# Value matmuls in blocks of four steps, two steps behind the scores, in a fused attention and expert layer

## The reference

```python
query = jnp.concatenate([q_nope, q_pe], axis=-1)
key = jnp.concatenate([k_nope, jnp.broadcast_to(k_pe, (B, H, S, ROPE))], axis=-1)
scores = jnp.einsum('bhsd,bhtd->bhst', query, key) * scale
attn = jax.nn.softmax(scores.astype(jnp.float32), axis=-1).astype(query.dtype)
out = jnp.einsum('bhst,bhtd->bhsd', attn, v)
```

## Time and profile before

| Stretch or engine | us |
|---|---|
| median of the timed runs | 2569.87 |
| span of the profiled execution | 2588.1 |
| TensorE busy in the span | 2303.3 (89%) |
| VectorE, ScalarE, GpSimd busy | 1390.3, 1375.7, 1380.6 |
| preparation, start to about | 178 |
| side work of head 0 alone, to about | 268 |
| attention loop, to about | 1896 |
| output projection, routing, experts, sum, to | 2588 |

### The profile page before, as it was taken

The page is one execution under the profiler, slowest core; times in us unless marked ns, Lnnn a source line. Parts: engine busy times, 40 slices in busy tenths (PEclk is TensorE's granted clock), DMA queues, the critical chain, the costliest instruction groups (busy, mean ns, idle before and its releaser), DMA issues. The chain is left out here.

```text
span 2588.1 us, 38846 instructions
## 1 busy us (share of the span) xinstructions
PE 2303.3 (89%) x10836; PEld 1411.5 (55%) x10836; DVE 1390.3 (54%) x2685; ACT 1375.7 (53%) x1915; POOL 1380.6 (53%) x810
## 2 busy tenths in 40 slices
PE   6887999999999999999999999999984565999980
PEld 3633555555555555555555555555563343777760
DVE  4527657567565575575665755756036224333327
ACT  3510566666666666666666666666832111333336
POOL 1000566666666766666666666666841464333331
PEclk9885899999999999999999999999995677999995
DMA  4216000000000000000000000000001564999978
GB/s 146 72 54 211 1 1 1 1 1 1 1 1 1 1 1 1 1 1 1 1 1 2 1 1 1 1 1 1 1 1 34 185 212 151 371 355 356 355 252 289
DMA packets 97037, 198.44 MB, mean 77 GB/s; under 512 B 13662, under 2 KB 59656, under 8 KB 96648
## 3 DMA queue, kind: packets, MB, share of 16 engines
q1 hardware_dynamic: 85384, 165.16, 19.0%
q0 software_dynamic: 11520, 31.52, 3.2%
HBM read 142.00 MB, written 54.64 MB: 76 GB/s over the span
## 5 line engine op out<-in xcount | busy, mean ns | idle before, releaser
L636 POOL TENSOR_TENSOR prob_lo<-prob,prob_hi 128x1024 f16<-128x1024 f32 x512 | 1118.1, 2185 | 591.9 <-ACT prob_hi L656 591.6
L654 ACT ACTIVATE prob<-p_s,prob_scale 128x1024 f32<-128x1024 f32 x512 | 570.6, 1114 | 622.3 <-PE p_s L806 622.3
L691 DVE TENSOR_REDUCE maxes<-p_m 128x1 f32<-128x512 f32 x1024 | 693.0, 690 | 292.5 <-PE p_m L775 282.9
L656 ACT ACTIVATE prob_hi<-p_s,prob_scale 128x1024 f16<-128x1024 f32 x512 | 566.9, 1107 | 0.0
L775 PE MATMUL p_m<-k_hi,q_hi 96*128 96x512 f32 x1024 | 443.4, 446 | 15.9 <-DVE maxes L691 12.3
L806 PE MATMUL p_s<-q_hi,k_hi 97*128 97x512 f32 x1024 | 371.8, 444 | 8.3 <-DVE q_hi L700 8.3
L806 PE MATMUL p_s<-q_lo,k_hi 97*128 97x512 f32 x1024 | 321.8, 395 | 0.0
L806 PE MATMUL p_s<-q_hi,k_lo 97*128 97x512 f32 x1024 | 321.0, 395 | 0.0
L775 PEld LDWEIGHTS p_m<-k_hi,q_hi 96*128 96x128 f32 x1024 | 194.9, 194 | 182.2 <-DVE maxes L691 134.3
L1510 PE MATMUL p_g<-w,rT 128*128 128x352 f32 x640 | 230.1, 484 | 39.1 <-issue 24.8
L806 PEld LDWEIGHTS p_s<-q_hi,k_hi 97*128 97x128 f32 x1024 | 175.5, 190 | 124.0 <-issue 110.0
(11 more groups left out here) (217 smaller groups left out, 2145.9 us busy)
## 6 DMA issues: line engine op xcount, KB each, us to landing
w<-in_experts SPq DMA_DIRECT2D x144, 608.0 KB
expert_rows<-zeros SPq DMA_DIRECT2D x64, 257.0 KB, 5.0
rows<-expert_rows SPq DMA_DIRECT2D x128, 128.5 KB
got<-ranked_out SPq DMA_DIRECT2D x16, 768.0 KB, 5.4
wqb<-in_wqb SPq DMA_DIRECT2D x16, 341.0 KB, 3.0
rows<-expert_rows SPq DMA_DIRECT2D x32, 128.0 KB
shared_out<-y SPq DMA_DIRECT2D x32, 128.0 KB
got<-shared_out SPq DMA_DIRECT2D x16, 256.0 KB, 7.1
```

Of the source, the lines that this page charges most:

```text
L636: gp.tensor_tensor(prob_lo[s % 4][:, :], prob[s % 2][:, :], prob_hi[s % 4][:, :], ALU.subtract).then_inc(lo_ready, 1)
L654: act.activation(prob[s % 2][:, :], p_s[s % 2][:, :], ACT.Exp, bias=prob_scale[:, :], scale=SCALE)
L656: act.activation(prob_hi[s % 4][:, :], p_s[s % 2][:, :], ACT.Exp, bias=prob_scale[:, :], scale=SCALE).then_inc(p_ready, 1)
L691: v.tensor_reduce(maxes[:, n:n + 1], p_m[n % 2][:, :], AX.X, ALU.max).then_inc(max_used, 1)
```

## The change

- `weigh` is issued for four steps at once. A head is eight groups; group g first issues the scores of steps 4g + 2 to 4g + 5, then `weigh` of steps 4g to 4g + 3. Scores of steps 32 and 33 are steps 0 and 1 of the next head. Before the first head, scores of steps 0 and 1 are issued by themselves.
- All side work lies at one of twelve slots of a group, one behind each part of the scores. Projections stand in the last slot of groups 0 to 3, maxima in groups 1 to 7 (8, 10, 10, 10, 10, 10, 6), turns in slot 4 of groups 0 and 4, rows 0 and 1 in slots 3 and 7 of group 6, rows 2 and 3 together in the last slot of group 7. Nothing but the four `weigh` stands between the last slot of a group and the first of the next.
- prob_hi and prob_lo have eight tiles instead of four.
- maxneg is reduced in two halves, each as soon as its 32 maxima are there; rows 0 and 1 wait for the first half only.
- c_hi and c_lo are made at the end of the keys' section in `mods_and_weights`, on VectorE, instead of at the start of `attention`.

```diff
+NB = 8
...
+            step(v.tensor_scalar(c_hi[:, :], caug[:, :], C_SCALE, None, ALU.mult))
+            v.scalar_tensor_tensor(out=c_lo[:, :], in0=caug[:, :], scalar=C_SCALE, in1=c_hi[:, :], op0=ALU.mult,
+                                   op1=ALU.subtract)
...
-        prob_hi = [sb(f"prob_hi{n}", 2 * QC, F16) for n in range(4)]
-        prob_lo = [sb(f"prob_lo{n}", 2 * QC, F16) for n in range(4)]
-        c_hi = sb("c_hi", T * CP, F16)
-        c_lo = sb("c_lo", T * CP, F16)
+        prob_hi = [sb(f"prob_hi{n}", 2 * QC, F16) for n in range(NB)]
+        prob_lo = [sb(f"prob_lo{n}", 2 * QC, F16) for n in range(NB)]
...
-        MAXIMA = (0, 0, 0, 0, 3, 4, 0, 2, 3, 3, 3, 4, 0, 2, 3, 4, 0, 2, 3, 3, 3, 3, 3, 3, 3, 3, 3, 3, 1, 0, 0, 0)
-        PROJECT = (1, 5, 11, 15)
-        assert sum(MAXIMA) == 4 * T and all(sum(MAXIMA[:s + 2]) <= 16 * c for c, s in enumerate(PROJECT))
-
-        def beside(first, last):
-
-            at = {}
-            for s in range(STEPS):
-                copy, turn, others, maxima = [], [], [], []
-                if s == 17 or (s == 1 and not first):
-                    copy = [("copy", 0 if s == 17 else 1)]
-                if s == 19 or (s == 3 and not first):
-                    turn = [("turn", 0 if s == 19 else 1)]
-                if not last:
-                    maxima = [("max", n) for n in range(sum(MAXIMA[:s]), sum(MAXIMA[:s + 1]))]
-                    others = [("project", c) for c in range(4) if PROJECT[c] == s]
-                    others += [("row", c) for c in range(4) if 28 + c == s]
-                at[s] = maxima[:2] + copy + maxima[2:] + turn + others
+        HEAD_USES = [("turn", 1), ("project", 0), ("project", 1), ("project", 2), ("project", 3), ("turn", 0),
+                     ("row", 0), ("row", 1), ("row", 2), ("row", 3)]
+        MAXIMA = (0, 8, 10, 10, 10, 10, 10, 6)
+        assert sum(MAXIMA) == 4 * T
+
+        def maxima_at(group):
+
+            first = sum(MAXIMA[:group])
+            count = MAXIMA[group]
+            at = [[] for _ in range(12)]
+            begin, end = {1: (4, 12), 7: (0, 6)}.get(group, (0, 12))
+            for n in range(count):
+                at[begin + n * (end - begin) // max(count, 1)].append(first + n)
             return at
 
+        def aside(group, slot, first, last):
+
+            if group == 0 and slot == 4 and not first:
+                return [("turn", 1)]
+            if group == 4 and slot == 4:
+                return [("turn", 0)]
+            if last:
+                return []
+            if group < 4 and slot == 11:
+                return [("project", group)]
+            if group == 6 and slot in (3, 7):
+                return [("row", slot // 4)]
+            if group == 7 and slot == 11:
+                return [("row", 2), ("row", 3)]
+            return []
+
...
-                if n == 4 * T - 1:
+                if n % (2 * T) == 2 * T - 1:
+                    half = n // (2 * T)
                     v.wait_ge(max_used, 64 * g + n + 3)
-                    v.tensor_reduce(maxneg[:, :], maxes[:, :].rearrange("p (t c) -> p t c", c=4), AX.X, ALU.max,
-                                    negate=True).then_inc(neg_ready, 1)
-                    v.wait_ge(neg_ready, g + 1)
+                    v.tensor_reduce(maxneg[:, half * 8:(half + 1) * 8],
+                                    maxes[:, half * 32:(half + 1) * 32].rearrange("p (t c) -> p t c", c=4), AX.X,
+                                    ALU.max, negate=True).then_inc(neg_ready, 1)
+                    v.wait_ge(neg_ready, 2 * g + half + 1)
...
-                v.wait_ge(o_mm, STEPS * h + 16 * half + 16 + 4)
+                v.wait_ge(o_mm, STEPS * h + 16 * half + 16 + NB)
...
+                for group in range(8):
+                    if group == 0 and not first:
+                        copy_out(1, h - 1)
+                    if group == 4:
+                        copy_out(0, h)
+                    at = maxima_at(group)
+                    for slot in range(12):
+                        if not last:
+                            for n in at[slot]:
+                                maximum(n, h + 1)
+                        for what in aside(group, slot, first, last):
+                            kind, c = what
+                            use = x_use(h, what, first, last)
+                            if kind == "project":
+                                project(c, h + 1, 1 - u, use)
+                            elif kind == "row":
+                                row(c, 1 - u, use)
+                            else:
+                                turn(c, h - c, use)
...
-            def scores(s, h, u, first, between):
+            def scores(part, s, h, u, rows_use):
 
                 half, kt = s // 16, s % 16
-                n = STEPS * h + s
-                if kt == 0:
-                    pe.wait_ge(x_used, x_base(h, first) + 2 * half - 1)
-                pe.wait_ge(p_ready, n + 1)
+                if part == 0:
+                    if kt == 0:
+                        pe.wait_ge(x_used, rows_use + 2 * half + 2)
+                    pe.wait_ge(p_ready, STEPS * h + s + 1)
                 keys = slice(kt * P, (kt + 1) * P)
-                for part, (kk, qq) in enumerate(((k_hi, q_hi), (k_hi, q_lo), (k_lo, q_hi))):
-                    if part and between:
-                        between.pop(0)()
-                    for j in range(2):
-                        c = 2 * half + j
-                        last = pe.matmul(p_s[s % 2][:, j * QC:(j + 1) * QC], kk[0:KS, keys],
-                                         qq[u][0:KS, c * QC:(c + 1) * QC], start=(part == 0), stop=(part == 2))
-                last.then_inc(s_mm, 1)
+                kk, qq = ((k_hi, q_hi), (k_hi, q_lo), (k_lo, q_hi))[part]
+                for j in range(2):
+                    c = 2 * half + j
+                    last = pe.matmul(p_s[s % 2][:, j * QC:(j + 1) * QC], kk[0:KS, keys],
+                                     qq[u][0:KS, c * QC:(c + 1) * QC], start=(part == 0), stop=(part == 2))
+                if part == 2:
+                    last.then_inc(s_mm, 1)
...
-                for s, todo in beside(first, last).items():
-                    maxima = [(lambda c=c: maximum(c, h + 1, 1 - u)) for kind, c in todo if kind == "max"]
-                    scores(s, h, u, first, maxima)
-                    if s >= 2:
-                        weigh(s - 2, h)
-                    elif not first:
-                        weigh(STEPS - 2 + s, h - 1)
-                    for m in maxima:
-                        m()
-                    for what in todo:
-                        kind, c = what
-                        if kind == "project":
-                            project(c, h + 1, 1 - u, x_use(h, what, first, last))
-                        elif kind == "row":
-                            row(c, h + 1, x_use(h, what, first, last))
-                        elif kind == "turn":
-                            turn(c, h - c, x_use(h, what, first, last))
+                own = x_use(None, ("row", 1)) if first else x_use(h - 1, ("row", 1), False)
+                for group in range(8):
+                    at = maxima_at(group)
+                    for slot in range(12):
+                        s, part = 4 * group + 2 + slot // 3, slot % 3
+                        if s < STEPS:
+                            scores(part, s, h, u, own)
+                        elif not last:
+                            scores(part, s - STEPS, h + 1, 1 - u, x_use(h, ("row", 1), first))
+                        if not last:
+                            for n in at[slot]:
+                                maximum(n, h + 1, 1 - u)
+                        for what in aside(group, slot, first, last):
+                            kind, c = what
+                            use = x_use(h, what, first, last)
+                            if kind == "project":
+                                project(c, h + 1, 1 - u, use)
+                            elif kind == "row":
+                                row(c, h + 1, use)
+                            else:
+                                turn(c, h - c, use)
+                    for s in range(4 * group, 4 * group + 4):
+                        weigh(s, h)
...
+            for s in range(2):
+                for part in range(3):
+                    scores(part, s, 0, 0, x_use(None, ("row", 1)))
```

More of the change, by code:

```diff
@@ L100, in program @@
             weff = sb(att, "weff", DK * H * KA)
-            caug = sb(att, "caug", T * CP)
+            c_hi = sb(att, "c_hi", T * CP, F16)
+            c_lo = sb(att, "c_lo", T * CP, F16)
             cosq = sb(att, "cosq", S)
@@ L518, in _, with attention @@
                 last.then_inc(ov_mm, 1)
-def attention(nc, hT, weff, caug, cosq, sinq, k_hi, k_lo, ident, slots_dram, cbar):
+def attention(nc, hT, weff, c_hi, c_lo, cosq, sinq, k_hi, k_lo, ident, slots_dram, cbar):
     st = ExitStack()
@@ L608, in x_use @@
```

(31 more changed lines are left out.)

24 lines of the change are left out of this document (9 added, 15 removed).

## The result

The changed kernel took 2586.45 us (median of four runs, 2582.96 to 2591.39) against 2567.91 us for the kernel before on the same chip: ratio 1.0078, with a 95% interval of 1.0057 to 1.0098. The forecast was 2583 us, with slower as the likeliest outcome (0.39).

The account below looks back on a forecast made before the run. TensorE's own queue order was taken to bound the attention loop. Transitions saved were expected to go into waits: 2569.9 + 8.4 (fifteen heads) + 5.3 (last head) = 2583 us, range 2528 to 2620.

Parts of the forecast that it names:

- The saving: In each head, three of four transitions between score and value matmuls go: 24 x 0.32 = 7.7 us.
- The chain of two score buffers: In a bare group, the third and fourth score steps wait for ScalarE's reading: 10.2 us instead of 9.44.
- VectorE after a projection: Behind the projections, L684 waits 0.2 to 1.0 us for GpSimd, once; the third maximum of the next group is late.
- Two rows in succession: Group 7: rows sharing one PSUM tile, row 3 starts 1.9 us after row 2 instead of 0.96; group takes 13.6.
- Group 6: Group with ten maxima and two rows inside the scores: TensorE bound, full gain, 12.7 us against 13.72.
- The head: Sum over eight groups: 102.65 us against 102.09, +0.56 a head, +8.4 us in the 15 heads with maxima.
- the missing 0.6 I leave on both sides: Per head, what the summed 102.1 us lacks against 102.7 measured, taken as equal in both kernels.
- The last head: Seven bare groups in the last head, each 0.76 us slower: +5.3 us.
- TensorE bound: Attention loop: TensorE stays bound or nearly, 2536 us, or 2448 if all waits are absent; chance 0.32.
- All three instructions blocked: After each projection, L684, L685 and L686 each wait for a whole GpSimd instruction: 2810 us; chance 0.15, nearly all at lower price.
- its milder form: After projections in four groups, one wait for GpSimd of up to 2.15 us instead of 0.2 to 1.0: +72, 2655 us.
- The 0.32 stays in the block: Value block: the 0.32 us belongs to value matmuls or their waits, not the transition; 2705 us at most; chance 0.05.

Follow-up runs that it names:

- the last kernel: Changed kernel with rows 2 and 3 apart, score buffer freed after its first reading, TensorE's loop written out and maxima placed again: 2472.47 us, ratio 0.9636.
- blocks of two: Changed kernel with weigh issued for two steps at once instead of four: 2672.2 us, ratio 1.0403; with side work placed for it 2553.75 us, ratio 0.9852.

## Why the prediction was right, and what it missed

**The saving.** Predicted: three of four transitions go, 7.7 us a head. With most waits taken away (the last kernel) a head is 97.05 against 102.07 of the kernel before without its loop, 5.0 less, and TensorE still waits 0.7 of it (10.4 us in fifteen heads). 0.4 more went back into rows (group 6 below). The remaining 1.6 or so of the 7.7 is not accounted for. In two of its groups the saving is there in full: group 5 (twelve maxima) takes 11.3 and group 3 (ten and a projection) 12.55, where the old order's prices give 12.27 and 13.49, 0.95 less each against the 0.96 of three transitions. Right in kind and, where nothing waits, in size.

**The chain of two score buffers.** Predicted: c waits 0.9 in a bare group, which takes 10.2 instead of 9.44. Measured 10.17 and waits of 0.84 and 0.35. Freeing the buffer one instruction earlier gives 9.26, so the cause is shown and not only the size.

**VectorE after a projection.** Predicted 0.9 to 1.7 us for the one instruction, and the two behind it unchanged: measured 0.75 to 1.47 (median 0.985), and 423 and 688 ns for the others. That the third maximum is late in groups 2 to 4 was shown by moving it. I had group 2 at 13.6 (13.44), group 4 at 13.2 (12.97): 0.16 and 0.23 too much.

**Two rows in succession.** Predicted a gap of about 0.9 and 13.6 for the group; 0.79 and 13.54, and 12.18 with the rows apart.

**Group 6.** Predicted 12.7, "full gain"; measured 13.17, with no wait in it. The price of a row, 0.96, was read where a value matmul stood ahead of it and scores behind it, so that it changed kinds there anyway. Now it stands inside the scores, and the timeline of after shows that it brings transitions of its own:

```profile
1085.25 0.40 PE L792 MATMUL p_m<-k_hi,q_hi 96*128 96x512 f32 x1
1085.58 1.03 PE L799 MATMUL p_x<-ident,maxneg 128*1 128x128 f32 x8
1086.54 0.72 PE L821 MATMUL p_s<-q_lo,k_hi 97*128 97x512 f32 x2
1087.10 0.40 PE L792 MATMUL p_m<-k_hi,q_hi 96*128 96x512 f32 x1
```

0.33 from the maximum to the row where another maximum is followed after 0.23, and 0.56 for the score pair behind it instead of 0.46: 0.2 more for each row, 0.4 of the 0.47. No run took this apart.

**The head.** +0.56 predicted, +0.57 measured. The errors of the groups cancel (-0.49 in groups 2 to 4, +0.47 in group 6), so the sum is better than its terms.

**The term that was mis-sized: "the missing 0.6 I leave on both sides".** I had left 0.6 us a head unexplained and called it equal in both kernels. But a head of before without a jump takes 102.01 (1002.36 to 1104.37, from one transpose of att_t to the same of the next head), which the sum of 102.1 meets: 102.7 is the length of a mean head. The 0.6 is the jump of TensorE's loop, once in two heads: 10.1 us in all before and 21.8 after, +11.7, almost as much as everything I had summed (+13.7). It was a term put at nothing without a reason. The two kernels with the loop written out show it. In the changed kernel TensorE stands still for 1.4 to 3.05 us at the jump, and behind the four longer gaps (1.93 to 3.05) its clock is granted at 0.50 for a stretch of 3 to 7 us, in which score pairs start 0.85 apart instead of 0.46. Before, the idle time at a jump was at most 1.7 us, and one of the six, of 1.66 us, was followed by such a stretch (a jump cost 1.2 to 3.2 us there, all told).

**The last head.** Predicted +5.3 (7 x 0.76); measured +9.8. Of it 4.3 are the bare groups: +0.73 in five of them, but only +0.35 in the two that hold a turn (10.17 against 9.82), since there the turn lies under c's wait. I had said so for group 0 and left it out of this sum. 5.7 go with stretches of low clock, 4.8 in the second and third group (13.40 and 11.72 instead of 10.17) and 0.9 behind the last scores; they are gone in the kernel with the loop written out, whose end is 0.3 shorter than that of before. No term of mine had them.

**Not seen at all:** head 0 gained 2.4, where the 3.6 us wait for q_lo is gone (I take it that group 0, without maxima, gives VectorE the time; no run shows it). With the 1.0 at the start it hides 3.4 of the 11.7 at the jumps. Predicted +13.7, measured +18.5 in the median, +26.1 in the trace. What the sum describes is the pair without the jumps, +11.0 in the traces. The jumps (11.7) and the low clock in the last head (5.7) stand in none of its terms, and why the median moved by less than the trace is not known. So the mechanism held, but that 2583 lies 3 us from 2586 is luck.

**The rivals.** TensorE bound: refuted, it is 94.9% busy, not 98. All three instructions blocked: refuted by 423 and 688 ns; its milder form is what the freed buffer brings about, one instruction at up to 2.54. The 0.32 stays in the block: refuted by the block's rows.

**Open.** Why the jump is longer in after (1.4 to 3.05 us against at most 1.7), and differs from trip to trip in one execution, no run settled. The traces point at the loading of instructions. In the eight traces with TensorE's loop there are 48 jumps, and at each a DMA packet of 16 KB of an instruction queue (q8) lands 1.5 to 2.4 us before TensorE starts again. In the last 5 us before that start the kernel before has one such packet at every jump, after has two. In the 16 jumps where two of them ran at the same time the idle time was 1.93 to 3.53 us, in the other 32 it was 1.05 to 1.98. With the loop written out such packets go on, and TensorE never stands still on "issue". That this is the cause is argued from these rows, not shown by a run. Nor does the length of a gap alone say whether the low clock follows: it followed 1.66 us in before, and not 2.54 us with the rows apart. Also open is why gaps of 0.84 and 0.35 lower the clock in the second and third bare group of after and not in the later ones.

## What to carry to other kernels

Issuing like with like saves the transitions only if the engine at the bound has something to do while the buffers turn round: place side work by when its operands and its buffers are ready, not evenly. When a period is summed and compared with a trace, put the unexplained remainder to its place before calling it equal on both sides; here it was a loop's jump, once in two periods, and it doubled. On a bound TensorE price every new gap twice, once as idle time and once as the stretch at half clock that may follow.

## What the runs showed of the hardware that was not expected

The jump of a loop of TensorE with a long body: 1.4 to 3.05 us of idle time in after, up to 3.53 with blocks of two; none with the loop written out. The granted clock fell to 0.50 (1.2 GHz) behind 21 of the 48 jumps traced, for 3 to 7 us. The Trainium skill (SBUF — State Buffer, "Who interferes with whom") has the rule by which VectorE waited for GpSimd, and the longest wait in these runs made 0.68 us into 2.54. Back-to-back f16 value pairs keep their 0.215 pace over twelve pairs, whatever semaphores stand between them.
